# Reciprocal root of the second layer's row scale: one power for all batches instead of one per batch

## What is computed

```python
x = L0_attn_x                                   # (8, 512, 128)
xn = _layernorm(x, axis=-1)
s = _L0_attn_ref(xn, ...)                       # causal linear attention
g = _silu(_L0_ffn_ref(xn, ...))                 # 8 experts, top 2
x = x + s * g
xn = _layernorm(x, axis=-1)
s = _L1_attn_ref(xn, ...)                       # starts with _rms(xn, g1)
g = _silu(_L1_ffn_ref(xn, ...))                 # 160 experts, top 8
x = x + s * g

def _rms(x, g):                                 # inside _L1_attn_ref
    return x * jax.lax.rsqrt(jnp.mean(x * x, axis=-1, keepdims=True) + EPS) * g
```

## Time and profile before

| | us |
|---|---|
| median of 3 runs | 1364.67 |
| lowest and highest run | 1358.96, 1369.6 |
| the profiled execution | 1365.29 |
| its span in the profile | 1363.5 |
| mean granted clock of TensorE over the span | 0.868 |

### The profile page before, as it was taken

One profiled execution on the slowest core, in us unless ns is written; L12 is line 12 of the kernel. 1 busy time (PEld: TensorE's weight loads), 2 busy tenths in 40 slices (PEclk: granted clock), 3 DMA queues, 4 the chain that ended last, 5 costly groups with the idle time before them and its releaser, 6 DMA issues. The chain is left out here.

```text
span 1363.5 us, 24768 instructions
## 1 busy us (share of the span) xinstructions
PE 997.6 (73%) x7728; PEld 804.2 (59%) x7728; DVE 878.3 (64%) x2899; ACT 630.9 (46%) x1431; POOL 679.2 (50%) x750
## 2 busy tenths in 40 slices
PE   1668789677777686786787659989687877969712
PEld 0656666556656565666566337679476765867611
DVE  3334677766766777777667535380759669687794
ACT  0314434324234244243333227787686676767711
POOL 2022335545645664664556450714656556665565
PEclk9988889789888898798898758999798989989865
DMA  7594753534633733634543937977556756657522
GB/s 240 161 322 140 264 165 98 167 135 152 216 113 114 243 133 97 210 127 128 174 143 110 373 104 225 320 228 215 157 172 194 228 156 201 205 168 230 148 88 60
DMA packets 178783, 242.88 MB, mean 178 GB/s; under 512 B 20016, under 2 KB 110832, under 8 KB 178032
## 3 DMA queue, kind: packets, MB, share of 16 engines
q1 hardware_dynamic: 158192, 199.55, 45.0%
q0 software_dynamic: 20480, 41.98, 10.6%
HBM read 129.73 MB, written 111.74 MB: 177 GB/s over the span
## 5 line engine op out<-in xcount | busy, mean ns | idle before, releaser
L1441 POOL DMA_INDIRECT y<-y_rows,idxy x256 | 259.4, 1013 | 203.7 <-DMA y<-y_rows,idxy 74.3
L1361 POOL DMA_INDIRECT rows<-xs,idx x256 | 253.6, 991 | 69.9 <-issue 65.4
L2034 DVE SCALAR_TENSOR_TENSOR V<-y,w8all,V 128x128 f32<-128x128 f32 x232 | 82.5, 356 | 114.6 <-PE V L1080 98.5
L977 PE MATMUL U<-ident,xg 128*128 128x128 f32 x576 | 98.6, 298 | 60.6 <-ACT xT L1240 46.4
L1653 DVE TENSOR_TENSOR att<-X,causal 128x512 f32<-128x512 f32 x128 | 82.3, 685 | 84.0 <-PE X L793 45.0
L977 PEld LDWEIGHTS U<-ident,xg 128*128 128x128 f32 x576 | 69.8, 151 | 85.8 <-issue 70.9
L1204 ACT ACTIVATE wd<-GY 128x384 f32<-128x384 f32 x120 | 59.0, 492 | 120.2 <-PE GY L903 120.1
L1341 POOL TENSOR_TENSOR ppause<-neg_half 128x1 f32<-128x1 f32 x80 | 16.8, 210 | 191.9 <-DVE idx L1813 98.5
L1240 ACT ACTIVATE xT<-U 128x512 f32<-128x512 f32 x144 | 86.4, 600 | 19.2 <-PE U L977 19.0
L1334 POOL TENSOR_TENSOR rs<-rs,neg_half 128x4 f32<-128x4 f32 x16 | 16.7, 1044 | 140.7 <-DVE rs L1479 140.7
L1829 DVE SCALAR_TENSOR_TENSOR terms<-pp,p 128x160 f32<-128x160 f32 x256 | 83.5, 381 | 0.8
(11 more groups left out here) (325 smaller groups left out, 2501.7 us busy)
## 6 DMA issues: line engine op xcount, KB each, us to landing
xg<-rows SPq DMA_DIRECT2D x144, 256.0 KB
y_rows<-ys SPq DMA_DIRECT2D x144, 256.0 KB
wd<-in_w0e SPq DMA_DIRECT2D x56, 576.0 KB, 5.5
rows<-zero SPq DMA_DIRECT2D x25, 1024.0 KB, 5.5
rows<-zero SPq DMA_DIRECT2D x4, 3072.0 KB, 14.7
wd<-rows SPq DMA_DIRECT2D x8, 1024.0 KB, 8.8
y_rows<-wd SPq DMA_DIRECT2D x24, 256.0 KB, 3.0
wd<-in_wd SPq DMA_DIRECT2D x1, 5120.0 KB
```

The lines of the kernel that those rows point to most:

```text
L977: last = nc.tensor.transpose(XT[:, q * P:(q + 1) * P], xg[:, k % RX, q, :], ident[:])
L1361: pool.indirect_dma_start(rows, bass.IndirectOffsetOnAxis(ap=idx[:, t * 8 + k:t * 8 + k + 1], axis=0), xs1[:, t, :], None)\
L1441: pool.indirect_dma_start(y8[:, i % RG, k, :], None, y_d[0:groups * Q * P, :], bass.IndirectOffsetOnAxis(ap=idxy[:, b, t * 8 + k:t * 8 + k ...
L2034: ins = nc.vector.scalar_tensor_tensor(o, y[:, k, :], w, o, ALU.mult, ALU.add)
```

## The change

The power of `r1` is no longer taken batch by batch. DVE's `res_norm` writes variance-times-square plus epsilon straight into the batch's column of `r1all`; the step `res_r1` is gone, with its copy and its wait. When the last batch's column is written, DVE counts `r1_in` up, and POOL takes the power of all 128x32 numbers in one instruction, in place. DVE waits for that (`r1_ready`) before it makes `nr1all`. `neg_half` grows from 16 to 32 columns, and `rsq_in` and `rsq_ready` count two events per batch instead of three.

```diff
-    rsq_in=3, rsq_ready=3,
+    rsq_in=2, rsq_ready=2,
...
-         7: ["place0c"], 9: ["res_r1"], 10: ["scatter0"], ...
+         7: ["place0c"], 10: ["scatter0"], ...
...
-        neg_half, pause, ppause = keep("neg_half", [P, H]), ...
+        neg_half, pause, ppause = keep("neg_half", [P, NB * T]), ...
...
             def s_res_norm(t):                         # POOL
-                rsqrt(r1[:])
+
+                if isinstance(here[0], int) and here[0] == NB:
+                    pool.wait_ge(once["r1_in"], 1)
+                    r1f = r1all[:].rearrange("p b t -> p (b t)")
+                    nc.gpsimd.tensor_tensor(r1f, r1f, neg_half[:], ALU.pow).then_inc(once["r1_ready"], 1)
...
                 link(nc.vector.tensor_tensor(ms1[:], ms1[:], mv[:, :, 1], ALU.mult))
                 join()
-                ask(nc.vector.tensor_scalar(r1[:], ms1[:], RMS_EPS, None, ALU.add))
-
-            def s_res_r1(t):
-                take()
-                link(nc.vector.tensor_copy(r1all[:, batch[0], :], r1[:]))
+                last = nc.vector.tensor_scalar(r1all[:, batch[0], :], ms1[:], RMS_EPS, None, ALU.add)
+                if isinstance(here[0], int) and here[0] == NB:
+                    last.then_inc(once["r1_in"], 1)
+                else:
+                    link(last)
...
             link(nc.vector.tensor_copy(hji[:], ej[:]))
+            dve.wait_ge(once["r1_ready"], 1)
             link(nc.vector.tensor_scalar(nr1all[:], r1all[:], -1.0, None, ALU.mult))
```

More of the change, by code:

```diff
@@ L141 @@
 STEPS = {0: ["res_comb"], 1: ["res_silu", "rank0"], 2: ["res_gate"], 3: ["res_add", "shift0"], 4: ["place0a"], 5: ["place0b"], 6: ["res_norm"],
-         7: ["place0c"], 9: ["res_r1"], 10: ["scatter0"], 11: ["xn1_T", "xn1T_copy"], 12: ["router1", "scatter_c"], 13: ["probs1"], 14: ["place0d"],
+         7: ["place0c"], 10: ["scatter0"], 11: ["xn1_T", "xn1T_copy"], 12: ["router1", "scatter_c"], 13: ["probs1"], 14: ["place0d"],
          15: ["topk1a"], 18: ["topk1b"], 20: ["topk1c"], 21: ["rank"],
@@ L146 @@
          76: ["router0", "exp0"], 79: ["topk0a"], 83: ["topk0b"]}
-LAST_STEPS = {0: ["res_comb"], 1: ["res_silu"], 2: ["res_gate"], 3: ["res_add", "shift0"], 6: ["res_norm"], 9: ["res_r1"],
+LAST_STEPS = {0: ["res_comb"], 1: ["res_silu"], 2: ["res_gate"], 3: ["res_add", "shift0"], 6: ["res_norm"],
               11: ["xn1_T", "xn1T_copy"], 12: ["router1", "scatter_c"], 13: ["probs1", "topk1a"], 14: ["topk1b"], 15: ["topk1c"], 16: ["rank"],
@@ L156 @@
         table.setdefault(at, [])[:0] = names
-RES = {"res_comb", "res_silu", "res_gate", "res_add", "res_norm", "res_r1", "xn1_T", "xn1T_copy", "router1", "probs1",
+RES = {"res_comb", "res_silu", "res_gate", "res_add", "res_norm", "xn1_T", "xn1T_copy", "router1", "probs1",
        "topk1a", "topk1b", "topk1c", "rank", "place_a", "place_b", "place_c", "place_d", "place_e", "place_f", "table", "weights_a", "weights_b",
@@ L334, in build @@
         silu_table = keep("silu_table", [1, 1], BF16)
-        neg_half, pause, ppause = keep("neg_half", [P, H]), keep("pause", [P, 1]), keep("ppause", [P, 1])
+        neg_half, pause, ppause = keep("neg_half", [P, NB * T]), keep("pause", [P, 1]), keep("ppause", [P, 1])
         r1all, nr1all = keep("r1all", [P, NB, T]), keep("nr1all", [P, NB, T])
@@ L434, in build @@
         once = {n: ctx.enter_context(nc.semaphore(n)) for n in ("const_ready", "zero_ready", "coef_in", "coef_exp", "neg_ready",
-                                                                "tab_ready", "row_ps", "row_ready", "first_done")}
+                                                                "tab_ready", "row_ps", "row_ready", "first_done", "r1_in", "r1_ready")}
         r0 = {n: ctx.enter_context(nc.semaphore(n)) for n in STREAM0}
@@ L1428, in _ @@
             pool.wait_ge(loaded["zeros7"], 32 * (NB - 2))
+            here[0] = NB
             others(SPAN0 * PAGES0, LAST_STEPS, {"res"})
```

## The result

| | before | after |
|---|---|---|
| median of 20 runs each, us | 1366.33 | 1372.54 |
| lowest and highest run, us | 1358.80, 1380.09 | 1361.94, 1383.22 |
| the profiled execution, us | 1365.29 | 1368.60 |
| its span, us | 1363.5 | 1366.7 |
| granted clock of TensorE over the span | 0.868 | 0.873 |

The changed kernel is slower: the ratio of the times is 1.0057, with a 95% interval of 1.0032 to 1.0081, so 4.4 to 11.1 us; the two medians are 6.2 us apart. Runs more than 1.5% above the fastest of their kernel are left out of all ratios and intervals here, but not out of the medians, so that a ratio can differ from that of two medians. The result is still inside the 1% that the prediction called "within", but not the 1364.5 us of its sum, nor its range, which ended at 1370.5.

What follows compares the result with a forecast made beforehand. No engine is full, so handovers between engines were taken to set the end. The terms summed to 0 on the path, bounds -4.7 and +1.0 us, from a median of 1364.67; forecast 1364.5 us, range 1358.0 to 1370.5.

Steps and rivals of the forecast that it cites:

- within: The case of a time within 1% (13.6 us) of the kernel before; chance 0.94.
- The seven powers that vanish: POOL, batches 0 to 6: 7.1 us of work goes, no scatter starts sooner; 0, bound 1.0 us in batch 6.
- The copy and its wait on DVE: DVE ahead of the gate product: at most 3.7 us saved, but nobody waits for that product; taken as 0.
- The argument, now linked: DVE ahead of `idx0n`: 0.75 us later in sum, at most 1.0, hidden in POOL's idle time; 0.
- Rival 3: Later `idx0n` delays POOL's layer 1 scatter 0.1 us per batch, the end by up to 1.0: 1365.7 us; chance 0.04.
- The one big power: POOL's 128x32 power after the last batch's argument: 7 us, between 1.0 and 8.1, nobody waits; 0.
- The same engines' ports: DVE beside POOL's small powers in batch 0: not held up through SBUF, so removing them gives DVE nothing.
- The wait of `probs1`: DVE's wait for PE's line 848: stays near 27.0 us, grows by about 2.2 if the saving runs into it.
- POOL's busy time: Falls by about 1 us if the big power takes 7 us, by 7 us if it takes 1.
- The signs of being wrong: Batch 0 to 6 distance changing over a few us, line 929 waiting for that gate product, last scatters after 850.
- The chances: For the whole kernel: faster by over 1% 0.03, within 1% 0.94, slower 0.03.

Runs made afterwards that it cites:

- scale_late: The changed kernel with the three DVE instructions that make the argument behind `idx0n` instead of ahead; 1367.38 us against 1367.56 before, ratio 0.9972.
- gate_later: The kernel before with four dependent one-column DVE writes behind the copy, so the gate product comes later; 1363.41 us against 1367.56, ratio 0.9986.
- no_copy_2: The kernel before, but POOL writes each small power straight into `r1all`, without DVE's copy and its wait; 1364.46 us against 1367.56, ratio 0.9996.
- layout_2: The kernel before with only `neg_half` widened from 16 to 32 columns; 1366.12 us against 1364.37, ratio 1.0016.
- after_2: The changed kernel run again without any edit, against the kernel before on the same chip; 1377.04 us against 1364.37, ratio 1.0075.
- own_sem_2: The changed kernel with the argument counted on its own semaphore in every batch instead of linked; 1372.34 us against 1364.37 before, ratio 1.0029.
- idx_later: The kernel before with four dependent one-column DVE writes ahead of the place computation in batches 0 to 5; 1371.35 us against 1367.56, ratio 1.0031.

## Why the prediction was wrong

Point by point, in the order of its steps.

- **The seven powers that vanish: right.** POOL lost them and no scatter of layer 1 started sooner. In batch 6 the scatters of an earlier batch do start 2.8 us sooner (3.77 instead of 6.52 us behind `x1n`; I had said up to 1.0, but the power had held POOL for its 1.0 us and for the 1.77 us that it waited for its argument), but scale_late does the same, and that trip takes 93.0 us against 93.6: nothing follows from it that these runs can tell.
- **The copy and its wait on DVE: right.** From `idx0n` to the gate product it is now 439.64 to 439.83, 0.19 us, and was 0.40. In front of the gate product 0.21 us went and 0.27 came. That this is hidden, gate_later and no_copy_2 show.
- **The argument, now linked: this step failed, twice.** First in size. I put the delay of `idx0n` at 0.12 us in a loop trip, from the 0.11 us between argument and `pause` growing to 0.20, and 0.03 for the address. It grew to 0.24 (438.25 and 438.49), and the write itself stands 0.31 us behind the multiply instead of 0.20: 0.24 of the 0.27 us, with the last 0.03 already there ahead of the multiply. In batches 0 and 5 it was 0.15. Second, and this is what cost the time, in what lies behind it. "What is left lies on POOL with its idle time: 0" is wrong. POOL's idle time stands *ahead* of `idx0n`: POOL is early there, waits, and starts when `idx0n` comes. A later `idx0n` only lengthens that wait at its far end. Behind it stand 20 issues at about 1.27 us each with hardly a gap, and the last of them end a wait of ACT and of DVE, and DVE's work a stop of PE. The idle time of the earlier trace rows was proof that POOL is released by `idx0n` directly, and I read it as cover. By the prediction's own rule, name what is queued behind the waiting instruction and who waits for that, the answer was in the trace of before: `ACT xs L1173 <- DMA rows<-xs,idx: 20.9, 6, 3.9`, and behind it `PE V L767 <- DVE kp L1628: 28.8, 6, 5.9`.
- **Rival 3 was the mechanism, at the wrong price.** It said that the scatter starts later and the end is late by that, at most 1.0 us, with a chance of 0.04. The place is right, and that the delay passes on one to one is not. From 0.27 us at `idx0n` it grows to 0.6 to 0.9 at the first layer-2 scatter and about 1.05 to 1.25 at ACT's copy (means over the loop in the three traces, against the one of before). In the loop's four trips that is 4.2 to 5.0 us. The three traces of the changed kernel have 384.8 us for these trips as mean, the four of kernels with an undelayed `idx0n` (before, layout_2, no_copy_2, gate_later) 377.9: 6.9 us more. The clock seems to be a part of that. The three stand at 1.2 GHz for 105.8 us of these trips as mean, the four for 90.5. A straight line through the 48 loop trips of the table's twelve traces gives 0.91 us of trip for 1 us at the copy and 0.26 us for 1 us at 1.2 GHz. Against the mean of those four, the copy of the three is 0.88 us late, so this makes 3.2 + 4.0 = 7.2 us. It is an estimate: no run changes one of the two alone. The ratio says 4.4 to 11.1 us over the whole kernel, 7.8 at its middle.
- **The one big power: right, its length wrong without harm.** No row gave it; I took 7 us between 1.0 and 8.1, and it measured 5.43. Nobody waits for it, as the profile after shows with what comes next on POOL:

```profile
808.97 5.43 POOL L1354 TENSOR_TENSOR r1all<-r1all,neg_half 128x32 f32<-128x32 f32 x1 [1.77 <-DVE r1all L1703]
...
849.72 0.19 POOL L1341 TENSOR_TENSOR ppause<-neg_half 128x1 f32<-128x1 f32 x1 [35.33 <-DVE idx L1818]
```

  That is 35.33 us idle behind it, and `nr1all` at 862.2 had no wait.
- **The same engines' ports: right for the question asked, which was too narrow.** The small powers did not hold DVE up, and without them DVE was not faster. But DVE and POOL do meet at another place: the issue of an indirect DMA that starts inside DVE's two-input `att` operation takes 1.48 us instead of 0.96. The Trainium skill (SBUF — State Buffer, section "Who interferes with whom") says that the order of issue decides who blocks. Here the row agrees, POOL being the second by 0.18 us. The same section tells of a probe in which DVE's `tensor_tensor` did not hold up a DMA, and infers that the two need different ports. The row speaks against that: `att` is such an operation, and the issue took 0.52 us longer beside it. The prediction had quoted the rule only for DVE as the one that waits.
- **The wait of `probs1`: right.** 27.0 us became 30.2, more than the 2.2 us that DVE's wait for the power had been: the saving ran into it. In batch 6 the wait grew from 2.46 to 3.56:

```profile
720.13 0.49 DVE L1712 TENSOR_TENSOR pp<-X,bias 128x320 f32<-128x320 f32 x1 [3.56 <-PE V L848]
```

- **POOL's busy time:** I expected about 1 us less, and it was 2.6 more. The long scatters are part of that.
- **The signs of being wrong.** In the result's profile none of the three gave a clear warning: from batch 0's `x1n` to batch 6's it was 559.6 us before and 561.9 after (569.7 in after_2), PE's line 929 did not wait for the gate product of that slot, and POOL turned to the last batch's scatters at 849.72, as against 850.08. They watched the places where the prediction had looked.
- **The chances.** "Within 1%" holds with the ratio; the range, 1358.0 to 1370.5, was too low at its upper end. It let the scatter of medians set that end, and counted the one mechanism that could go past it at 1.0 us.

Layer 2, too, is 4.2 us longer in the profiled execution of after (from `x1n` of the last batch, at 804.8 and 803.8, to the end). One pair of executions can't tell that from their scatter: this stretch takes 558.7 to 572.5 us in the table's twelve traces, and is longest in scale_late, and a single loop trip of the changed kernel took 98.8 us in one execution and 93.3 in another. What is left between the 6.9 us of the loop and the ratio's 7.8 lies within the intervals and stays open.

**A better version.** scale_late keeps what the change brings, one power, no copy, no second wait, and starts `idx0n` 0.44 us sooner than before. On the chip that ran both, its ratio is 0.7% below that of the change, and its median 0.6%. Against the kernel before, two comparisons give 0.9972 and 0.9980, with 1 inside each interval at its upper end, and medians 0.2 and 1.8 us lower: a gain over the kernel before isn't shown.

## What to carry to other kernels

Where an engine waits for another's result and then starts at once, its idle time says that it is exactly as late as that result; only idle time *behind* its work is cover. Follow the queue behind the waiting instruction to the engines that wait for its last entry, and from them to the one that the others wait for, before a delay of tenths of a microsecond is written down as nothing. And when a removed step hands its remains to an earlier place in an in-order list, look for a place behind the instruction that releases another engine: three small instructions, moved by three slots, made some 8 us here.

## What the runs showed of the hardware

- A power on POOL costs mostly by its columns: 1.01 us for 128x4, 5.43 us for 128x32.
- An indirect DMA issue of POOL of 0.96 us took 1.48 when it started 0.18 us into a 0.82 us DVE operation with two inputs from SBUF, and 0.96 when it started 0.11 us ahead of one of 0.83 us. Other traces give the steps between: 1.60 us when 0.06 us into it (layout_2, own_sem_2), 1.25 at 0.40 (idx_later) and 1.13 at 0.54 (after). Each ends some 1.66 us behind the start of DVE's operation, so it is longer by what was left of about 0.7 us of it.
- In the loop trip shown, TensorE's granted clock fell to 1.2 GHz in a stop of PE of 5.30 us before and 6.36 us after, and was back at 2.4 GHz by 477.9 and by 484.5 us; the same six matmuls took 0.83 us at the higher and 1.49 us at the lower level.
- Inside the loop, a write whose address comes from a register stands 0.31 us behind the instruction it depends on, instead of 0.20.
- The same program took 1364 to 1368 us on three chips and 1705 and 1731 us on two others, and an edit's sign turned round between them (1.0057 and 0.9889). A change of half a per cent should be measured on more than one chip.
